# Silu on ScalarE in place of tanh, with VectorE's sum-and-product step left out, in a two-layer attention and expert kernel

## What is computed

```python
# layer 0: 9 experts, hidden width 352
h = jax.nn.silu(x_flat @ ew1[e].T) * (x_flat @ ew3[e].T)
out = out + cw[:, e:e + 1] * (h @ ew2[e].T)
# layer 1: 8 experts and a shared one, hidden width 176
g = jnp.einsum('th,ehi->eti', x, w_gate)
u = jnp.einsum('th,ehi->eti', x, w_up)
eo = jnp.einsum('eti,eih->eth', jax.nn.silu(g) * u, w_down)
so = jax.nn.silu(x @ sw_gate) * (x @ sw_up) @ sw_down
```

## Time and profile before

| | us |
|---|---|
| median of 3 runs | 1865.59 (1862.56 to 1866.32) |
| the profiled execution | 1863.21 |
| its span, first to last instruction | 1861.5 |
| TensorE busy | 1488.8 (80%) |
| VectorE busy | 1194.4 (64%) |
| ScalarE busy | 896.3 (48%) |
| GpSimd busy | 726.9 (39%) |

### The profile page before, as it was taken

The page is one execution under the profiler, slowest core; times in us unless marked ns, Lnnn a source line. Parts: engine busy times, 40 slices in busy tenths (PEclk is TensorE's granted clock), DMA queues, the critical chain, the costliest instruction groups (busy, mean ns, idle before and its releaser), DMA issues.

```text
span 1861.5 us, 34997 instructions
## 1 busy us (share of the span) xinstructions
PE 1488.8 (80%) x13168; PEld 851.4 (46%) x13168; DVE 1194.4 (64%) x2460; ACT 896.3 (48%) x2074; POOL 726.9 (39%) x1135
## 2 busy tenths in 40 slices
PE   4178788888987888887988788888888879788966
PEld 3123463336633574335733465335743357334834
DVE  4177367557876578656776578665786567765734
ACT  4157326562366524663266633665246722665231
POOL 3235215632266223652156331662236521563051
PEclk8689889898999999998999999999999989999987
DMA  7410140003200040002300041000400022000000
GB/s 212 75 28 2 37 61 19 1 2 75 44 1 2 23 74 23 2 1 50 52 19 2 7 73 39 1 2 27 70 6 1 2 53 44 2 2 8 10 1 4
DMA packets 49754, 53.69 MB, mean 29 GB/s; under 512 B 5802, under 2 KB 38964, under 8 KB 49588
## 3 DMA queue, kind: packets, MB, share of 16 engines
q1 hardware_dynamic: 49588, 51.45, 14.0%
HBM read 38.98 MB, written 12.46 MB: 28 GB/s over the span
## 4 chain that ended last, share of the span: by engine, by line
PE 38%; DMA 26%; DVE 12%; ACT 10%; POOL 6%; issue 5%; SPq 2%; ACTq 0%; POOLq 0%; another core or an unknown queue 0%; DVEq 0%
DMA k_parts<-big 16%; DMA kst<-k_parts 7%; PE ob L663 7%; PE b L649 6%; ACT probs L942 5%; DVE mx L1117 5%; PE a L635 4%; PE b L555 3%; DMA k1st<-k_parts 3%; DVE mx L1139 2%; POOL big L1388 2%; ACT big L948 2%; PE ob L504 2%; PE b L685 2%; PE a L791 2%
## 5 line engine op out<-in xcount | busy, mean ns | idle before, releaser
L1117 DVE TENSOR_REDUCE mx<-a 128x2 f32<-128x802 f32 (+1 forms) x512 | 489.3, 986 | 278.0 <-PE a L635 275.6
L942 ACT ACTIVATE probs<-b 128x512 f32<-128x512 f32 (+1 forms) x896 | 459.0, 564 | 151.8 <-PE b L649 135.9
L663 PE MATMUL ob<-probs,vaug 128*9 128x256 f32 (+1 forms) x3328 | 284.1, 392 | 3.6 <-ACT oT L884 3.6
L1371 POOL TENSOR_TENSOR big<-iotab,idx_lo 128x512 bf16<-128x512 bf16 x256 | 274.1, 1093 | 7.7
L987 ACT ACTIVATE big<-a 128x256 f32<-128x256 f32 (+2 forms) x304 | 116.1, 382 | 324.3 <-PE a L792 321.5
L649 PE MATMUL b<-big,kst 64*128 64x256 bf16 (+1 forms) x1664 | 173.5, 278 | 106.9 <-ACT big L948 48.0
L635 PE MATMUL a<-kst,qa 64*128 64x401 bf16 (+1 forms) x1024 | 175.6, 344 | 78.2 <-SPq L474 33.7
L1234 DVE SCALAR_TENSOR_TENSOR big<-big,a 128x256 f32<-128x256 f32 (+2 forms) x304 | 127.1, 418 | 128.0 <-ACT big L987 126.2
L1352 POOL CAST qst<-nm 128x4 bf16<-128x4 f32 x64 | 15.6, 244 | 409.8 <-DVE nm L1104 409.0
L1319 POOL TENSOR_TENSOR rstd<-veps,neg_half 128x2 f32<-128x2 f32 x32 | 22.6, 705 | 367.8 <-DVE veps L1035 367.7
L649 PEld LDWEIGHTS b<-big,kst 64*128 64x128 bf16 (+1 forms) x1664 | 63.2, 95 | 220.4 <-ACT probs L942 107.9
(11 more groups left out here) (262 smaller groups left out, 2435.1 us busy)
## 6 DMA issues: line engine op xcount, KB each, us to landing
kst<-k_parts SPq DMA_DIRECT2D x96, 200.1 KB
k_parts<-big SPq DMA_DIRECT2D x24, 400.2 KB, 14.5
ctx_sb<-in_ctx SPq DMA_DIRECT2D x8, 768.0 KB
k1st<-k_parts SPq DMA_DIRECT2D x96, 32.0 KB
k_parts<-kpart SPq DMA_DIRECT2D x24, 64.0 KB, 1.6
kst<-in_L_ffn_w SPq DMA_DIRECT2D x1, 1408.0 KB
x<-in_x SPq DMA_DIRECT2D x8, 128.0 KB, 2.2
out<-x SPq DMA_DIRECT2D x8, 128.0 KB, 8.0
```

What stands on the lines that cost most here:

```text
L663: m = pe.matmul(ob[q:q + V1, 0:NQ], vaug[0:kn, c, 2 * p + hh, :], probs[0:kn, (2 * g + hh) % NPS, (c % 2) * NQ:(c % 2 + 1) * NQ], start=(j ...
L942: act.activation(probs[0:kn, (2 * n + hh) % NPS, 0:w], bs[(e + hh) % 3][0:kn, 0:w], ACT.Exp).then_inc(f_read, 1)
L1117: dve.tensor_reduce(mx[:, p % 2, s, :, j], bank[:, :].rearrange("p (h k) -> p h k", h=2)[:, :, 0:w], AX, ALU.max, negate=True).then_inc(m_ ...
L1371: m = pool.tensor_tensor(onehot[:, own % 2, q:q + QG, :], iotab[:, :].unsqueeze(1).to_broadcast([P, QG, P]), idx_lo[:, QG * n:QG * (n + 1) ...
```

## The change

ScalarE applies Silu to the gate's PSUM bank instead of tanh of half of it, and VectorE multiplies that by up at once. The tile `gt`, its semaphore and the 304 executions of its instruction are gone; `hu` now lies where `gt` was. VectorE's wait for `th` stands ahead of the hidden tile of the step before, as it stood ahead of `gt`. From step 3 on ScalarE waits for `hu` of three steps ago instead of `gt`. Since Silu has no factor 0.5 to make up for, the factor goes from 0.5 to 1.0 in the routing weights and the doubling in the shared expert's weight is left out. TensorE's, GpSimd's and SyncE's instructions are the same.

```diff
-        th, gt, hu = (big[:, 5632 + 768 * k:5632 + 768 * (k + 1)].rearrange("p (n q) -> p n q", q=NQ) for k in range(3))
+        th, hu = (big[:, 5632 + 768 * k:5632 + 768 * (k + 1)].rearrange("p (n q) -> p n q", q=NQ) for k in range(2))
...
                         act.wait_ge(gu_ready, u + 1)
                         if u >= 3:
-                            act.wait_ge(gt_done, u - 2)
-                        act.activation(th[0:n, u % 3, :], gu_bank[u % 3][0:n, 0:NQ], ACT.Tanh, scale=0.5).then_inc(th_ready, 1)
+                            act.wait_ge(hu_done, u - 2)
+                        act.activation(th[0:n, u % 3, :], gu_bank[u % 3][0:n, 0:NQ], ACT.Silu).then_inc(th_ready, 1)
...
-                    st.do(dve.tensor_scalar(lz[:, :, 8:9], le[:, :, 8:9], 1.0, 2.0, ALU.add, ALU.mult))
+                    st.do(dve.tensor_scalar(lz[:, :, 8:9], le[:, :, 8:9], 1.0, None, ALU.add))
...
-                st.do(dve.scalar_tensor_tensor(out=wtop[:, :, :], in0=top[:, :, 0:2], scalar=0.5, in1=wrec[:, :].unsqueeze(2).to_broadcast([P, NS, 2]),
+                st.do(dve.scalar_tensor_tensor(out=wtop[:, :, :], in0=top[:, :, 0:2], scalar=1.0, in1=wrec[:, :].unsqueeze(2).to_broadcast([P, NS, 2]),
...
                         dve.wait_ge(th_ready, u + 1)
-                        dve.scalar_tensor_tensor(out=gt[0:n, u % 3, :], in0=th[0:n, u % 3, :], scalar=1.0, in1=g[0:n, 0:NQ],
-                                                 op0=ALU.add, op1=ALU.mult).then_inc(gt_done, 1)
                         if u >= 1 and (B or u >= 3):
                             for v in (range(u - 1, u) if B or u > 3 else range(3)):
                                 hidden(v)
-                        dve.wait_ge(gt_done, u + 1)
-                        dve.tensor_tensor(hu[0:n, u % 3, :], gt[0:n, u % 3, :], g[0:n, NQ:2 * NQ], ALU.mult).then_inc(hu_done, 1)
+                        dve.tensor_tensor(hu[0:n, u % 3, :], th[0:n, u % 3, :], g[0:n, NQ:2 * NQ], ALU.mult).then_inc(hu_done, 1)
```

More of the change, by code:

```diff
@@ L199, in build @@
         le_ready, cwp_ready = ([sem(f"{n}{k}") for k in range(2)] for n in ("le_ready", "cwp_ready"))
-        gu_ready, th_ready, gt_done, hu_done, cb_ready, hid_ready, down_done = (
-            sem(n) for n in ("gu_ready", "th_ready", "gt_done", "hu_done", "cb_ready", "hid_ready", "down_done"))
+        gu_ready, th_ready, hu_done, cb_ready, hid_ready, down_done = (
+            sem(n) for n in ("gu_ready", "th_ready", "hu_done", "cb_ready", "hid_ready", "down_done"))
         kf_ready, kp_ready, kres_ready, kf1_ready, kp1_ready, kres1_ready = (
```

## The result

The changed kernel takes 1899.41 us (median of 4 runs, 1895.86 to 1903.02); the kernel before took 1865.95 us beside it (4 runs, 1862.56 to 1866.49). The ratio is 1.0183, 95% interval [1.0155, 1.0211]: slower by 33.5 us. The forecast was 24.5 us slower, 1890.0, with a range of 1878 to 1910; the time lies inside the range and outside the 1885 to 1896 that the forecast gave itself without its rivals.

A forecast was written before the change was run, and what follows sets the result against it. TensorE's compute path was taken to set each pass's end, not the key-copy DMA. Passes 1 to 6 (23.4), 7 (+1.4), 0 (-0.45) and 8 (+0.1) gave 24.5 us slower, 1890 us, range 1878 to 1910.

The forecast's parts named there:

- The count and the price of a load: ScalarE, wherever Silu follows Exp or the reverse: 31 function-table loads added, taken at 1.28 us each.
- The rival of a double price: ScalarE empties before each load, so a switch costs twice the row: 1926 us in all; chance 8%.
- The rival of free loads: Loads hidden in ScalarE's idle time or short, leaving only the removed steps' saving: 1858 us, faster; chance 5%.
- First Silu: Load ahead of a pass's first Silu, partly absorbed by ScalarE's idle time and a removed VectorE step: +0.45 us.
- Routing's pair with the removed step: Two loads around the routing's Exp, +2.83 us a pass, less 0.34 for VectorE's removed step on the way out.
- Tail: End of the feed-forward stage: VectorE's last sum-and-product step goes, -0.34 us a pass.
- GpSimd stayed ahead of VectorE: Rival: VectorE's first routing step gets ahead of GpSimd's split, saving about 1 us per pass, 1884 us; chance 12%.
- First Exp: Load ahead of attention's first Exp, where TensorE waits for ScalarE and nothing hides it: +1.30 us a pass.
- the case that the attention stage takes part of it up: The first Exp's delay is partly recovered later in attention, up to 9 us; shares a 12% chance with VectorE's rival.
- rival of the clock: Longer TensorE waits at 637 and 723 drop its clock, 3 us each in six of fourteen places: 1908 us; chance 15%.
- The sum by passes: Passes 1 to 6 lose 3.90 us each, pass 7 1.4, pass 8 0.1; pass 0 gains 0.45; sum 24.5 us.
- What the removed step is worth: VectorE's sum-and-product gone: 0.34 us behind the routing and 0.34 at the tail of passes 1 to 6.

The follow-up runs named there:

- e6: e5 with one-column Exp and Silu activations that start the remaining loads early, where ScalarE idles; 1852.48 us, ratio 0.998 to the kernel before.
- e3: The changed kernel with six filler matmuls on TensorE behind the first scores of each pass, the load kept; 1895.34 us, ratio 1.014.
- e1: The changed kernel with tanh kept in the activation: VectorE's step is out, no table is switched; 1849.51 us, ratio 0.993.
- e11: The kernel before, tanh and step kept, with e9's 28 filler matmuls in TensorE's wait for routing; 1860.54 us, ratio 1.001.
- e9: e6 with 28 filler matmuls in TensorE's wait for routing in passes 1 to 7; 1852.18 us, ratio 0.995.
- e8: The kernel before with a 1344-column copy on ScalarE ahead of attention's first Exp of each pass, no table switched; 1880.13 us, ratio 1.010.
- e2: The kernel before with Silu in place of tanh and VectorE's step kept, so all 31 switches are in; 1917.71 us, ratio 1.028.
- e5: The changed kernel with layer 0's routing gate by Tanh instead of Exp and one VectorE routing step less, 17 loads left; 1882.22 us, ratio 1.012.
- e4: The changed kernel with a one-column Exp at the end of each feed-forward stage, taking the load off attention's first Exp; 1882.83 us, ratio 1.010.
- e7: The kernel before with only layer 0's routing gate by Tanh and one VectorE routing step less; 1858.39 us, ratio 1.002.

## Why the prediction was right, and which term was short

**The count and the price of a load** were right: 31 loads, 1.28 us each, the next activation 0.02 us behind. The rival of a double price fell with that. The Trainium skill (ScalarE: Activation LUTs, What ACT_TABLE_LOAD costs) adds 1380 ns of draining to the 1283 ns; these rows show the 1283 and no second part, neither behind the load nor, at 650.15, ahead of it. The rival of free loads fell too; but ScalarE's idle time, which spoke for it, is there: e6 hides all loads in it, by starting them early.

**First Silu**, forecast +0.45: +0.40. **Routing's pair with the removed step**, +2.94 together with the first Silu at the point where TensorE resumes: +2.98. **Tail**, -0.34: from +2.98 to +2.79, -0.19. The stage: +2.60 forecast, +2.62 in the mean of passes 2 to 6 (84.39 against 81.77), but that the two agree so closely is luck: one of the five, pass 5, owes some 2.3 us to a clock that stayed up at the stage's start, and the other four stand at +2.8 to +3.2. GpSimd stayed ahead of VectorE, so that rival fell, by 0.06 us.

**First Exp**, +1.30: the step that was mis-sized. The wait grew by 1.27, as worked out. Its direct price at the stage's end is only 0.69 in the one pass that shows it (e3's pass 4): the case that the attention stage takes part of it up held there, for 0.6 us. On the other side the clock fell 12 to 15 us into every pass from 1 to 7, and the stage grew by 3.9 in the mean of passes 2 to 6. The prediction had this as its rival of the clock, with six of fourteen places and 3 us for each. It named the right place (723, where the wait becomes 2.1) and a wrong one (637, where the wait became 1.90: the clock stayed up in passes 2 and 3, and where it fell, in passes 4 and 6, it did so in place of the low stretch at the stage's start, and the stage was no longer); and it priced one low stretch behind the wait, which costs 0.3 us, and not those that stand 65 to 125 us further on, with which the stage is 3 to 7 us longer.

**The sum by passes.** Of the 39.8 us, passes 2 to 6 hold 32.8, where 19.5 were forecast; pass 7 holds 7.0 (1.4 forecast), again by its attention stage (140.9 against 134.3); pass 1 gained 0.4 (3.9 forecast as a loss), because before it had 25 us of low clock in its attention stage and now has 13; pass 5 lost only 0.8, for the same reason in small (before 9.7 us low, 136.8 long). Pass 0 gave 1.8 instead of 0.45; pass 8, from its first product on, took 1.8 instead of 0.1, with 26 us low instead of 20. The start of the program adds 0.5. So luck has a part in the number: passes 2 to 7 lost 19 us more than the sum said, and passes 0 and 1 came out 6 us better than it said, pass 1 by its clock. The range held because it took in the rival of the clock; of the signs of being wrong that the prediction named, the one of more stretches at 0.50 came true.

**What the removed step is worth**, -0.68 a pass: 0.5 to 1.0 at a like clock in e1, 0.9 between e11 and e9. That is the forecast, some 5 us in all. The other 11 of e1's 16 us stand for the most part beside less low clock, 2.2 us in each feed-forward stage that is without its low stretch at the start; as e8's pass 3 has such a stage with the step in place, it is not shown that they come from the step.

**What stays open.** At least 8 us of work stood at the low clock in 20 of 20 attention stages with the 2.0 to 2.1 us wait (passes 2 to 6 of the changed kernel, e2, e5 and e8) and in 12 of 35 with the wait of 0.83 (6 of 25 in before, e1, e4, e6 and e7, but 6 of 10 in e9 and e11), and also in 4 of 5 where e3's fillers had cut the longer wait to 0.7. That a delay of the first Exp matters is shown (e8); that it acts by the length of TensorE's wait alone is not, since e3 contradicts it. Neither is it shown what decides between a pass with a second fall and one without: pass 1 of the kernel before had 25 us low behind a wait of 0.83.

## What to carry to other kernels

Before a function is exchanged on ScalarE, list which others run between its uses, and where each load would stand: where another engine waits for the next activation the load comes on top of that wait (1.28 of it at the first Exp here), in idle time it delays nothing, and a one-column activation moves it there. Price a longer wait of TensorE twice, once by its length and once by what runs at 1.2 GHz afterwards, and look for the latter through the whole stage, not only right behind the wait. Before a gain of several edits is put down to one of them, run the others on the kernel before. Compare stages at an equal clock before crediting a gain or a loss to an edit; and let fillers run only in passes that have the wait they are meant for.

## What the runs showed of the hardware that was not expected

- TensorE's clock can fall with nothing but short waits ahead. In the changed kernel's pass 3 it stood at 0.60 from 729 to 733 and at 0.55 from 794 to 801, with no wait over 0.94 us in the 50 us ahead of the second. The kernel before had the same short waits in that pass and kept 1.00.
- Time lost early in an attention stage can be partly made up: in e3's pass 4, 1.27 us at its start were 0.69 at its end.
- Tanh shares a table with Exp (the kernel before switches none) and with Silu (e5's routing switches none), while Silu and Exp share none. The Trainium skill (ScalarE: Activation LUTs, Table sets: the hidden batching unit) has tanh in the set of exp, as the trace shows, and advises to batch by set. The function in two sets is the bridge that made e5 possible.
- VectorE's 18-column step took 3.19 us under GpSimd's 3.21-us instruction, which had started only 0.06 us ahead, and 0.17 us in pass 7, where that instruction is missing.
